# A fused two-layer kernel: the first stage in another order, and products of ones in two pauses

## What is computed

```
x  = L0_attn_x                                  # (4, 256, 256)
xn = layernorm(x)
s  = attention0(xn, Wq, Wk, Wv, Wo)             # rope, causal softmax, 16 heads of 16
g  = silu(experts0(xn))                         # 16 experts, the 4 best of each token
x  = x + s * g
xn = layernorm(x)
s  = attention1(xn, ...)                        # linear attention: elu(q) (elu(k)^T v)
g  = silu(experts1(xn) + shared(xn))            # 32 experts, the 4 best of each token
x  = x + s * g
```

## Time and profile before

| | us |
|---|---|
| median of 3 runs | 414.98 (413.81 to 415.04) |
| profiled execution | 413.56 |
| its span, first to last instruction | 411.8 |

### The profile page before, as it was taken

One profiled execution on the slowest core, in us unless ns is written; L12 is line 12 of the kernel. 1 busy time (PEld: TensorE's weight loads), 2 busy tenths in 40 slices (PEclk: granted clock), 3 DMA queues, 4 the chain that ended last, 5 costly groups with the idle time before them and its releaser, 6 DMA issues.

```text
span 411.8 us, 9630 instructions
## 1 busy us (share of the span) xinstructions
PE 395.2 (96%) x3059; PEld 291.1 (71%) x3059; DVE 315.9 (77%) x1070; ACT 231.7 (56%) x583; POOL 211.5 (51%) x205
## 2 busy tenths in 40 slices
PE   8999999999999999799998899999999999999995
PEld 4765797797787787466666678468778776566684
DVE  5886788887988556679999988766788972545895
ACT  3273244344344446789999953645777767524731
POOL 2104487776774210588785410177777720677710
PEclk9899999999999999889999999999999999999999
DMA  7948888889899998279688874034666644333322
GB/s 232 392 179 274 289 267 293 287 283 315 286 331 296 296 310 273 72 174 206 159 196 217 224 281 164 1 92 125 180 188 184 186 133 139 88 98 108 90 69 73
DMA packets 41073, 82.84 MB, mean 201 GB/s; under 512 B 6928, under 2 KB 26000, under 8 KB 40384
## 3 DMA queue, kind: packets, MB, share of 16 engines
q1 hardware_dynamic: 29792, 60.59, 44.2%
q0 software_dynamic: 9600, 19.93, 19.5%
q10 hardware_dynamic: 1632, 1.71, 1.3%
HBM read 65.42 MB, written 14.68 MB: 195 GB/s over the span
## 4 chain that ended last, share of the span: by engine, by line
PE 87%; DVE 9%; issue 2%; DMA 1%; ACT 1%; ACTq 0%; DVEq 0%
PE ps L1258 14%; PE ps L1197 8%; PE ps L1478 7%; PE ps L1297 6%; PE ps L1401 5%; PE ps L1224 5%; PE ps L1376 4%; PE ps L1025 3%; PE ps L1041 3%; PE ps L1489 3%; PE ps L1253 3%; PE ps L1183 3%; PE ps L1044 2%; PE ps L1235 2%; PE ps L1289 2%
## 5 line engine op out<-in xcount | busy, mean ns | idle before, releaser
L588 POOL DMA_INDIRECT til<-xn_rows,gidx x64 | 64.0, 1000 | 84.5 <-PE ps L1235 36.8
L911 ACT ACTIVATE til<-til,mxs 128x128 f32<-128x128 f32 (+1 forms) x128 | 49.0, 452 | 0.0
L1258 PEld LDWEIGHTS ps<-til,experts 128*128 128x128 f32 x384 | 45.3, 192 | 4.8 <-DVE til L1823 2.4
L1258 PE MATMUL ps<-til,experts 128*128 128x128 f32 x384 | 47.8, 278 | 0.7 <-issue 0.3
L763 ACT ACTIVATE til<-ps 128x256 f32<-128x256 f32 x40 | 15.3, 383 | 57.2 <-PE ps L1235 57.1
L1947 DVE CUSTOM_DVE_ANT_0 til<-ps,cst 128x128 f32<-128x128 f32 (+1 forms) x128 | 37.9, 353 | 6.5 <-PE ps L1376 5.8
L812 ACT ACTIVATE til<-ps,wtile 128x256 f32<-128x256 f32 x88 | 38.8, 469 | 4.3 <-PE ps L1226 2.4
L1199 PE MATMUL ps<-xn,til 128*64 128x192 f32 x192 | 33.8, 329 | 0.0
L1197 PE MATMUL ps<-experts,til 128*64 x192 | 33.7, 329 | 0.0
L1401 PE MATMUL ps<-cst,til 128*128 128x128 f32 x192 | 28.9, 289 | 4.5 <-DVE til L1956 3.6
L1297 PE MATMUL ps<-experts,til 128*128 x128 | 33.1, 381 | 0.0
(11 more groups left out here) (278 smaller groups left out, 1038.5 us busy)
## 6 DMA issues: line engine op xcount, KB each, us to landing
experts<-in_gu SPq DMA_DIRECT2D x32, 512.0 KB, 5.2
sorted_rows<-til SPq DMA_DIRECT2D x88, 128.0 KB, 2.2
att<-in_gu SPq DMA_DIRECT2D x16, 512.0 KB, 6.1
experts<-in_gu SPq DMA_DIRECT2D x8, 768.0 KB, 5.3
experts<-in_dn SPq DMA_DIRECT2D x4, 1024.0 KB, 11.6
experts<-in_dn SPq DMA_DIRECT2D x8, 384.0 KB, 6.4
experts<-att SPq DMA_DIRECT2D x44, 32.0 KB
xr<-in_x SPq DMA_DIRECT2D x2, 512.0 KB, 4.3
```

Of the source, the lines that this page charges most:

```text
L588: po.indirect_dma_start(to, None, xn_dram[s.n], bass.IndirectOffsetOnAxis(ap=gidx[:, at:at + 1], axis=0))\
L911: ins = ac.activation(pr[h % len(pr)][:, cols], pr[h % len(pr)][:, cols], ACT.Exp, bias=mxs[:, h % len(pr), tt:tt + 1], scale=-1.0)
L1258: mm = pe.matmul(ps[:, b0, m * P:(m + 1) * P], gw[n][:, k * w + m * P:k * w + (m + 1) * P], xgT[:, j % 2, k, :], start=(k == 0), stop=(k = ...
```

## The change

x is loaded in three parts (tiles 0 and 1, 2 and 3, 4 to 7), and VectorE's statistics of the first half wait for two parts in turn. The value weights Wv become a transfer of their own, right behind the router's weights and on the same semaphore, so router product 0 waits for both; Wq and Wk come later. The value products are issued between the turns, three steps behind (`NARROW_LAG`), on TensorE and in ScalarE's loop, and the five products of ones ahead of turn 4 are gone. Value product 6 comes before the first counts, 7 before the third; the first half of Q/K product 0 comes before the last count. The places come one Q/K product later in the order than before. The opening fill has 15 products instead of 18. As the attention begins, six products of ones stand before the second scores, behind a wait for the weighing of all but the last tile of experts, and five before the turns of the second pair of heads.

```diff
+        NARROW_LAG = 3
+        X_PARTS = ((0, 2), (2, 4), (4, 8))
...
-            sp.dma_start(xr[:, 0:4, :], x_rows[:, 0:4, :]).then_inc(s_x[0], 16)
-            sp.dma_start(cst[:, 0:P], consts[:, 0:P]).then_inc(s_id, 16)
-            sp.dma_start(xr[:, 4:8, :], x_rows[:, 4:8, :]).then_inc(s_x[1], 16)
+            for part, (t0, t1) in enumerate(X_PARTS):
+                sp.dma_start(xr[:, t0:t1, :], x_rows[:, t0:t1, :]).then_inc(s_x[part], 16)
+                if part == 1:
+                    sp.dma_start(cst[:, 0:P], consts[:, 0:P]).then_inc(s_id, 16)
             sp.dma_start(wqkv_sb[:, :, 3 * D:3 * D + E0], wr0).then_inc(s_wr, 16)
+            sp.dma_start(wqkv_sb[:, :, 2 * D:3 * D], wqkv0[:, :, 2 * D:3 * D]).then_inc(s_wr, 16)
             sp.dma_start(cst[:, P:], consts[:, P:C_END]).then_inc(s_cst, 16)
             sp.dma_start(rb0_sb[:, :], rb0.partition_broadcast(P)).then_inc(s_rb, 16)
-            sp.dma_start(wqkv_sb[:, :, 0:3 * D], wqkv0).then_inc(s_wqkv, 16)
+            sp.dma_start(wqkv_sb[:, :, 0:2 * D], wqkv0[:, :, 0:2 * D]).then_inc(s_wqkv, 16)
...
                         ac.dma_start(xn_dram[0][i * P:(i + 1) * P, :], xn[:, i, :]).then_inc(s.xn_stored, 16)
-                    for i in range(NTT):
+                        if i >= NARROW_LAG:
+                            narrow(s, i - NARROW_LAG)
+                    for i in range(NTT - NARROW_LAG, NTT):
                         narrow(s, i)
...
                 if i == 0:
-                    pe.wait_ge((s_wr, s_wqvu1)[s.n], (16, 32)[s.n])
+                    pe.wait_ge((s_wr, s_wqvu1)[s.n], 32)
...
-                if i == 0 and s.n == 0:
-                    pe.wait_ge(s_wqkv, 16)
...
                     for i in range(NTT + 1):
-                        if i == 4:
-                            dense(5, 5)
                         if i < NTT:
                             turn(s, i)
                         if i >= 1:
                             router(s, i - 1)
-                    narrow(s, 0)
-                    narrow(s, 1)
+                        if i >= NARROW_LAG:
+                            narrow(s, i - NARROW_LAG)
+                    narrow(s, 6)
                     count(s, 0)
                     count(s, 1)
-                    narrow(s, 2)
+                    narrow(s, 7)
                     count(s, 2)
+                    wide(s, 0, (0,))
                     count(s, 3)
-                    for i in range(3, NTT):
-                        narrow(s, i)
...
-                wide(s, 0)
                 if s.n == 0:
+                    wide(s, 0, (1,))
+                    wide(s, 1)
                     for i in (0, 1, 2):
                         place(s, i)
-                    wide(s, 1)
+                    wide(s, 2)
                     for i in (3, 4, 5):
                         place(s, i)
-                    wide(s, 2, (0,))
+                    wide(s, 3, (0,))
                     place(s, 6)
                     place(s, 7)
                     tile_experts(s)
-                    wide(s, 2, (1,))
-                    wide(s, 3)
+                    wide(s, 3, (1,))
...
-            dense(18, 2)
+            dense(15, 2)
...
             def turn_probs(p, j):
+                if p == 1:
+                    dense(5, 6)
...
+            pe.wait_ge(L[0].y_ready, NT0 - 1)
+            dense(6, 6)
             run_pairs([(0, 2, lambda n, j: scores(n, j) if n >= 1 else None), (2, 1, turn_probs), (8, 4, turn_rows),
...
-                ve.wait_ge(s_x[h], 16)
-                for i in range(4 * h, 4 * h + 4):
-                    ins = ve.bn_stats(bnst[:, i, :], xr[:, i, :])
+                for part, (t0, t1) in enumerate(X_PARTS):
+                    if t0 // 4 == h:
+                        ve.wait_ge(s_x[part], 16)
+                        for i in range(t0, t1):
+                            ins = ve.bn_stats(bnst[:, i, :], xr[:, i, :])
```

More of the change, by code:

```diff
@@ L281, in build_program @@
         psf = ps[:, :, :].rearrange("p b n -> p (b n)")
-        s_x = [sem(f"x_in{h}") for h in range(2)]
+        s_x = [sem(f"x_in{h}") for h in range(3)]
         s_cst, s_wr, s_bias, s_wqkv, s_dn0, s_w1, s_wqvu1, s_small1, s_tab1 = map(sem, (
@@ L1135, in route @@
                     tile_experts(s)
-                    wide(s, 2, (1,))
-                    wide(s, 3)
+                    wide(s, 3, (1,))
                 else:
+                    wide(s, 0)
                     wide(s, 1)
```

## The result

| | before | after |
|---|---|---|
| median of six runs, us | 414.53 (412.35 to 415.04) | 419.25 (416.63 to 423.46) |
| profiled execution, us | 413.56 (span 411.8) | 420.34 (span 418.6) |
| ratio of times | | 1.0112, 95% interval 1.0057 to 1.0167 |

The account below looks back on a forecast made before the run. TensorE was taken as the bound, with 87% of the chain of waits. First stage +3.2 (1.5 later, 1.7 for clock) and fills -1.7 gave +1.5 on 414.98: 416.5 us; range 412.9 to 420, the forecast's own 415.9 to 417.3.

Parts of the forecast that it names:

- signs: What would show it right: TensorE idle over 1.5 us before turn 4, over 3 before the places; ranks read at 22-24.
- first rival: Turns: tile 4 is ready after value product 0, turn 4 at 10.4, ranks at 21.1; 413.2 us, faster; chance 0.17.
- third rival: Turns: the clock falls there too, at least 3.3 us at half clock; about 419 us; chance 0.17.
- x in three loads: Start: the first row statistics end 0.70 us earlier, moving the first turn from 7.46 to 6.76.
- The wait on the value weights: Router product 0, now also waiting for the value weights: cost 0 to 0.5 us, taken as 0.
- The ranks: End of the ranks on TensorE: done at 22.7, 3.2 us later, not held by VectorE's choices.
- The pause before the places: TensorE idles 3.6 us between ranks and places; the clock falls, costing 1.7 us, bounds 0 to 3.3.
- The second rival: The pause before the places costs no clock; net -0.2, 414.8 us, no change; chance 0.15.
- The step that failed: Ranks to first expert product: one Q/K product fewer, 1.72 us, and 2 us of cover leave it 1.5 later at full clock.
- R: The moment the ranks are done, 19.52 us in the kernel before.
- The fills: Attention's start: eleven products of ones in two pauses keep the clock up, -1.7 us, ends 0 and -1.9.
- The fourth rival: Attention's start: the fills bring nothing back; 418.2 us; chance 0.09.

Follow-up runs that it names:

- run with the square root first: The changed kernel with ScalarE issuing the square root for tiles 4 to 7 ahead of its copy of value product 0: 416.34 us, ratio 1.0074.
- mended one: Changed kernel with that square root ahead, value weights waited on only at value product 0, and Q/K product 2 ahead of the places: 413.27 us, ratio 0.9989.

## Why the prediction was right, and where it was off

*The direction was right, and so were the links up to the places.* The second square root stands behind the copy of value product 0 (11.53 and 11.81), TensorE is idle before turn 4, the ranks are late and VectorE waits for them, TensorE is idle before the places, the clock is 0.50 behind that, and 1.00 in the attention, with the second to the fourth scores 3.79 and 3.78 us apart. Three of the signs missed in size: TensorE idles for 1.23 us before turn 4 (over 1.5 named) and 2.84 before the places (over 3), and the ranks are read at 25.19 (22 to 24). The run with the square root first makes the first rival's condition true (turn 4 with no idle time, ranks at 21.45 where that rival had 21.1), and even so it was slower (1.0074): the rival's 413.2 also needed full clock at the places and a covered gather, and had neither.

*The time lies in the range in part by luck.* The loss is +4.7 us where the sum had +1.5, and 419.25 is outside the forecast's own 415.9 to 417.3. The range held it because it reached to 420 for the third rival.

*x in three loads*, -0.70, was right in mechanism: turn 0 at 6.72 in the run without fills and 6.77 in the mended one, against 6.76. In the profiled execution of the change it was 7.14. What was missed is that the opening fill can end later than the data: "the fill ends 0.64 sooner" holds only where the clock has risen as early as in the execution that was read.

*The wait on the value weights* was taken at 0 between 0 and 0.5; it measured 0.2 to 0.7. The bounds came from the constants, which GpSimd has by 8.11; "less data is ahead" doesn't bring a transfer home by 7.6, when router product 0 is ready for it.

*The ranks*: 22.7 predicted, 22.84 in the execution with full clock in the turns, 25.19 in the profiled one. There turn 4 was 0.68 later and TensorE ran at a clock of 0.60 from 12.8 to 16.2 and of 0.96 from 16.3 to 25.0: 3.4 x 0.40 + 8.7 x 0.04 = 1.7 us, which is the rest of the 2.35. The third rival therefore came true in some executions and not in others. VectorE's choices moved more than the 1.3 us allowed, by 3.6 in the profiled execution (last mark at 19.01 before, 22.61 after), but as predicted they don't hold the ranks: VectorE waits 2.30 us for them.

*The pause before the places* was predicted at 3.6 us and was 2.84; its cost in clock at 1.7 between 0 and 3.3, and was 1.4, 2.4 and 2.8 (lists behind the ranks, less the 10.13 without a fall). The second rival (no clock lost) is out, by the run with fills in that place.

*The step that failed* is the one that turned +3.2 at the ranks into +1.5 at the first expert product: "Afterwards it has one Q/K product fewer to do than now", with lists that "keep some 2 us of cover". The cover was 1.0 us, and 1.0 is lost again behind the wait for the gather, so the ranks' delay and the clock's go through nearly in full: TensorE's own products don't set the first expert product, and one Q/K product fewer, 1.72 in the sum, takes nothing off. In the run without fills: +3.28 at the ranks, +4.72 at the lists, +4.57 at the first expert product, where +3.2 was predicted (1.5 and 1.7 for the clock). In the profiled execution of the change the same chain gives +5.63, +8.44 and +8.55. The prediction named that case, "the first tile would move with R, by 3.2 instead of 1.5", and put no chance on it. With it the forecast would have been 414.98 + 3.2 + 1.7 - 1.7 = 418.2, against 419.25 measured.

*The fills*: -1.7 predicted, -2.05 from the first scores to the fourth, and -1.3 (-2.1 to -0.4) or -2.3 (-3.2 to -1.4) in time for the eleven and the six alone, from their ratios. The fourth rival is out. Beside it stood the Trainium skill, page "TensorE: Matmul & The Clock Gate", section "Why this matters for your kernels", by which the clock drops mid-kernel behind a long idle gap. The pair of runs decides against it as the only cause here: the longest pause at that place was 1.42 us, filling it took the clock from 0.50 to 1.00, and taking the fills out of the changed kernel brought 0.50 back for over 10 us. Five of the eleven products were not needed.

## What to carry to other kernels

Work that nobody needs yet is a good filler only where neither the engine that does it nor the one that copies its results out has something urgent queued behind: here the copy of a value product stood ahead of a square root, and the products ahead of the ranks. Cover is to be measured from the transfer's own landing to its reader, not from an idle engine in between, and a reader that has begun to wait may lose time behind the wait as well (1.0 us here). A pause that is short enough to look harmless can still cost granted clock; a few products without a reader, put in front of work that has to wait anyway, are a cheap way to find out.

## What the runs showed of the chip that was not expected

The clock falls in a given place in some executions of a program and not in others. The kernel before and the one with the fills alone have the same program up to the attention. The two value products behind the turns, the first of which begins at 14.54 and 14.48, ran at 0.50 in the profiled execution of the one and at 1.00 in that of the other:

```profile
13.00:16.00 3.00, 3.00 (x20) 2.65 (x20) 2.69 (x20) 1.10 (x3) 0.00 (x0) 1.00 1.03 423
16.00:25.00 9.00, 7.65 (x41) 5.70 (x40) 7.91 (x40) 3.41 (x10) 0.00 (x0) 1.00 0.99 403
```

Of the eighteen runs of the kernel before that were timed beside the fills alone, fourteen had a mean clock of 0.986 to 0.991 and took 413.1 to 415.2 us, and four had 0.995 to 0.998 and took 411.3 to 412.0. The opening fill's products pass from 0.43 to 0.22 us each at 4.6 in the execution of before, at 4.1 in that of the mended kernel and at 6.7 with x in three loads and fifteen products (read from the distances of their starts; the column of the clock shows 1.00 there all the while). The Trainium skill, page "TensorE: Matmul & The Clock Gate", section "Part 1: The HAM clock gate (the "warmup" mystery)", says that the number of products at the low clock at a kernel's start differs from run to run; these traces agree, and show the same in the middle of a kernel.

A fall that comes behind a pause need not end soon: the stretches shown, 6.1 us before the expert tiles and 10.2 us in the attention of the run without fills, are at 0.50 throughout, with TensorE busy for 5.79 and 9.93 us of them.
